# All 48 expert chunks of an image in one stretch behind its attention

## The reference, cut to what matters

```python
# x: 16 images of 192 channels x 32 x 32, so 1024 tokens of 192 channels an image
x = x + L0_conv_ref(_gn(x), ...)     # gated row and column scans, group norm before
t = _to_tokens(x)
t = t + L1_attn_ref(_ln_t(t), ...)   # 6 heads of 32, window of 33 keys, and a first token that sees all and is seen by all
t = t + L1_ffn_ref(_ln_t(t), ...)    # 4 experts, 192 -> 768 -> 192 with gelu; the best 2 of 4 weighted by softmax gates
x = _from_tokens(t, x)
```

## Time and profile before

| | us |
|---|---|
| median of 3 runs (4031.06 to 4038.34) | 4033.3 |
| span of the profiled execution | 4009.3 |
| TensorE busy | 3540.4 (88%) |
| VectorE busy | 2293.3 (57%) |
| ScalarE busy | 1733.3 (43%) |
| mean granted TensorE clock | 0.932 of full |

### The profile page before, as it was taken

The page is one execution under the profiler, slowest core; times in us unless marked ns, Lnnn a source line. Parts: engine busy times, 40 slices in busy tenths (PEclk is TensorE's granted clock), DMA queues, the critical chain, the costliest instruction groups (busy, mean ns, idle before and its releaser), DMA issues.

```text
span 4009.3 us, 68583 instructions
## 1 busy us (share of the span) xinstructions
PE 3540.4 (88%) x24347; PEld 2432.0 (61%) x24347; DVE 2293.3 (57%) x6031; ACT 1733.3 (43%) x4063; POOL 144.9 (4%) x132
## 2 busy tenths in 40 slices
PE   0698989999899899989989998999989989998998
PEld 0466665666666566666656666566666656666665
DVE  3445655656656465655646466564665646565554
ACT  0132634536253363625436263452625336362542
POOL 0000000000000000000000000000000000000000
PEclk9569989999999899999999899998999989999989
DMA  3100000000000000000000000000000000000000
GB/s 48 46 13 4 13 8 13 7 3 14 8 13 8 13 6 4 14 8 14 8 13 6 3 13 8 13 7 2 14 8 13 8 13 6 4 14 8 5 5 9
DMA packets 68306, 44.26 MB, mean 11 GB/s; under 512 B 58909, under 2 KB 59970, under 8 KB 66372
## 3 DMA queue, kind: packets, MB, share of 16 engines
q10 hardware_dynamic: 8416, 30.67, 2.5%
q1 hardware_dynamic: 59492, 8.53, 1.7%
HBM read 21.07 MB, written 12.84 MB: 8 GB/s over the span
## 4 chain that ended last, share of the span: by engine, by line
issue 60%; PE 25%; DVE 8%; POOL 2%; ACT 2%; SPq 0%; DMA 0%; ACTq 0%; POOLq 0%; DVEq 0%
PE PSUM L1137 3%; PE PSUM L1213 2%; PE PSUM L1310 2%; PE PSUM L1134 1%; PE PSUM L1217 1%; PE PSUM L1215 1%; ACT HF L583 1%; PE PSUM L1194 1%; PE PSUM L1195 1%; PE PSUM L1196 1%; PE PSUM L1197 1%; PE PSUM L1198 1%; PE PSUM L1174 1%; DVE X L840 1%; PE PSUM L1230 1%
## 5 line engine op out<-in xcount | busy, mean ns | idle before, releaser
L583 ACT ACTIVATE HF<-PSUM,B 128x512 f32<-128x512 f32 x768 | 509.1, 685 | 732.3 <-PE PSUM L1198 672.0
L1213 PE MATMUL PSUM<-W2H,HHI 128*128 128x192 f16 x3072 | 770.2, 251 | 23.0 <-DVE HLO L828 23.0
L1217 PE MATMUL PSUM<-W2H,HLO 128*128 128x192 f16 x3072 | 765.1, 249 | 0.0
L1215 PE MATMUL PSUM<-W2L,HHI 128*128 128x192 f16 x3072 | 764.8, 249 | 0.0
L825 DVE TENSOR_SCALAR HHI<-HF 128x512 f16<-128x512 f32 x768 | 323.3, 421 | 673.4 <-ACT HF L583 672.5
L828 DVE SCALAR_TENSOR_TENSOR HLO<-HF,HHI 128x512 f16<-128x512 f32 x768 | 531.6, 692 | 26.4
L622 ACT ACTIVATE PS<-PSUM,NMX 94x126 f32<-94x126 f32 x1056 | 366.0, 357 | 114.6 <-DVE NMX L867 77.7
L1213 PEld LDWEIGHTS PSUM<-W2H,HHI 128*128 128x128 f16 x3072 | 313.1, 102 | 132.9 <-issue 41.9
L1230 PE MATMUL PSUM<-KBD,QT 96*94 96x378 f32 x704 | 312.6, 528 | 41.3 <-issue 39.7
L1215 PEld LDWEIGHTS PSUM<-W2L,HHI 128*128 128x128 f16 x3072 | 303.9, 99 | 40.2 <-issue 14.1
L867 DVE TENSOR_REDUCE NMX<-PSUM 94x3 f32<-94x378 f32 x352 | 188.4, 544 | 231.9 <-PE PSUM L1233 207.2
(11 more groups left out here) (233 smaller groups left out, 5542.4 us busy)
## 6 DMA issues: line engine op xcount, KB each, us to landing
XR<-in_x ACTq DMA_DIRECT2D x16, 768.0 KB, 5.6
out_dram<-X ACTq DMA_DIRECT2D x32, 384.0 KB, 2.3
GUP<-TGU SPq DMA_DIRECT2D x256, 8.0 KB, 1.8
TGU<-HSP SPq DMA_DIRECT2D x128, 8.0 KB, 1.8
XG<-HSP SPq DMA_DIRECT2D x128, 8.0 KB, 1.8
HF<-in_w ACTq DMA_DIRECT2D x3, 384.0 KB, 3.3
X<-in_w ACTq DMA_DIRECT2D x3, 384.0 KB, 3.2
XG<-XN SPq DMA_DIRECT2D x16, 64.0 KB, 2.3
```

The lines of the kernel that those rows point to most:

```text
L583: act.activation(HF[:, n % 2, :], PSUM[:, 4 + n % 2, :], ACT.Gelu, scale=1 / (X_UP * W_UP), bias=B1[:, ek:ek + 1]).then_inc(s["gelu_done"], 1)
L1213: pe.matmul(dst, HHI[:, n % 2, tok], W2H[:, e * HK + k, :], start=False, stop=False, skip_group_check=True)
L1215: pe.matmul(dst, HHI[:, n % 2, tok], W2L[:, e * HK + k, :], start=False, stop=False, skip_group_check=True)
L1217: mm = pe.matmul(dst, HLO[:, n % 2, tok], W2H[:, e * HK + k, :], start=False, stop=(k == HK - 1), skip_group_check=True)
```

## The change

All chunks of image i move into `experts(i, *side)`, behind `attention(i)`; `attention` loses its argument `before` and everything that stood under it. `STEPS` becomes one or two side steps a chunk for 8 chunks and one for each later chunk; a new helper `finish` runs out what is left of the generators behind the last chunk. The gates of the second half are made at chunk 26, its route exponential at chunk 24, the first store at chunk 28, the second behind the last chunk. `LINKS_FIRST` is a count of VectorE's own semaphore steps and follows from the order.

```diff
-        STEPS = [(1, n % 2) if n < 17 else (2, 1) for n in range(NCHUNK // 2)] + [(1, 1)]
+        STEPS = [(1, n % 2) if n < 8 else (1, 0) for n in range(NCHUNK)] + [(1, 1)]
+        def finish(works):
+            works = list(works)
+            while works:
+                works = [work for work in works if next(work, works) is not works]
 # ScalarE
-                    if before:
-                        if b == 1:
-                            store(i - 1, 1)
-                        for n in (2 * b, 2 * b + 1):
-                            gelu(i - 1, NCHUNK // 2 + n)
+            def experts(i, *side):
+                step(side, STEPS_AHEAD)
+                for n in range(NCHUNK):
+                    if n == NCHUNK // 2:
+                        route_exp(i, 0)
+                    gelu(i, n)
+                    if n == NCHUNK // 2 + 4:
+                        store(i, 1)
+                    step(side, sum(STEPS[n]))
+                finish(side)
+                store(i, 0)
 # VectorE: split, add_expert and gates leave attention in the same way
+                for n in range(NCHUNK):
+                    if n > 1 and n % HK == 1:
+                        add_expert(i, n // HK - 1)
+                    if n == NCHUNK // 2 + 2:
+                        gates(i, 0)
+                    split(i, n)
+                    step(side, sum(STEPS[n]))
+                add_expert(i, 2 * E - 1)
+                finish(side)
 # TensorE
-                    if before:
-                        ffn1(i - 1, half0 + 2 * b)
-                        ffn1(i - 1, half0 + 2 * b + 1)
                     if b >= 1:
-                        if before:
-                            ffn2(i - 1, half0 + 2 * b - 2)
                         values(2 * b - 2)
                         values(2 * b - 1)
-                        if before:
-                            ffn2(i - 1, half0 + 2 * b - 1)
+            def experts(i, *side):
+                step(side, STEPS_AHEAD)
+                for n in range(NCHUNK + 1):
+                    if n < NCHUNK:
+                        ffn1(i, n)
+                    step(side, STEPS[n][0])
+                    if n >= 1:
+                        ffn2(i, n - 1)
+                    step(side, STEPS[n][1])
+                finish(side)
 # all three engines
-                attention(i, True, True)
-                experts(i, 1, rest(i), conv(i + 1))
+                attention(i, True)
+                experts(i, rest(i), conv(i + 1))
```

More of the change, by code:

```diff
@@ L34 @@
 NCHUNK = NHALF * E * HK
-LINKS_FIRST, LINKS = 78, 61
+LINKS_FIRST, LINKS = 89, 61
 X_UP, W_UP, H_UP = 1024.0, 64.0, 8.0
@@ L608, in route_exp, with attention @@
                 act.activation(SE[:, tiles, :], SC[:, tiles, :], ACT.Exp).then_inc(s["route_exp"], 1)
-            def attention(i, before, following):
+            def attention(i, following):
                 if following:
                     load(i + 1)
-                if before:
-                    route_exp(i - 1, 0)
-                for b in range(NB + 1):
-                    if b < NB:
-                        for n in (2 * b, 2 * b + 1):
[L618 to L625, removed]
-                    if before:
-                        if b == 1:
-                            store(i - 1, 1)
-                        for n in (2 * b, 2 * b + 1):
-                            gelu(i - 1, NCHUNK // 2 + n)
+                for b in range(NB):
+                    for n in (2 * b, 2 * b + 1):
+                        act.wait_ge(s["max_done"], at("max_done", i, n + 1))
+                        if n >= 2:
+                            act.wait_ge(s["pT_done"], at("pT_done", i, n - 1))
+                        for h in range(HH):
+                            e = act.activation(PS[:, n % 2, h, :], PSUM[0:QS, n % 2, h * KS:(h + 1) * KS],
+                                               ACT.Exp, bias=NMX[:, b, n % 2, h:h + 1],
+                                               accum_out=DEN[:, b, n % 2, h:h + 1])
+                        e.then_inc(s["exp_done"], 1)
                 for n in (0, 2):
@@ L653, in rest @@
                 yield
-            def experts(i, half, *side):
+            def experts(i, *side):
                 step(side, STEPS_AHEAD)
-                for n in range(NCHUNK // 2):
-                    gelu(i, (1 - half) * NCHUNK // 2 + n)
+                for n in range(NCHUNK):
[4 more added lines that the diff above has]
+                        store(i, 1)
                     step(side, sum(STEPS[n]))
+                finish(side)
+                store(i, 0)
             def load_weights(n):
@@ L673, in _ @@
                     load_weights(n // 3 + 2)
-            attention(0, False, True)
-            experts(0, 1, rest(0), conv(1))
+            attention(0, True)
+            experts(0, rest(0), conv(1))
             with act.Fori(1, B - 1) as i:
-                attention(i, True, True)
-                experts(i, 1, rest(i), conv(i + 1))
[L679 to L684, removed]
+                attention(i, True)
+                experts(i, rest(i), conv(i + 1))
+            attention(B - 1, False)
+            experts(B - 1, rest(B - 1))
             for half in range(2):
@@ L842, in add_expert, with attention @@
                 last.then_inc(s["ffn_added"], 1)
-            def attention(i, before, following):
-                half0 = NCHUNK // 2
+            def attention(i, following):
                 def copy_turned(n):
@@ L889, in attention @@
                         add_image(i + 1)
-                if before:
-                    split(i - 1, NCHUNK - 2)
                 for n in (1, 3):
@@ L916, in attention @@
                 norm_tokens(X2, range(4, 8)).then_inc(s["xn2_ready"], 1)
-                if before:
-                    add_expert(i - 1, 2 * E - 1)
                 low_parts(i, 1)
@@ L1283, in attention @@
                     turn_output(n)
-                if before:
-                    ffn2(i - 1, NCHUNK - 2)
                 pe.wait_ge(s["oT_copied"], at("oT_copied", i, 4))
@@ L1288, in attention @@
                     output(i, tp)
-                if before:
-                    ffn2(i - 1, NCHUNK - 1)
                 if following:
@@ L1367, in rest, with experts @@
                 yield
-            def experts(i, half, *side):
-                n0 = (1 - half) * NCHUNK // 2
+            def experts(i, *side):
                 step(side, STEPS_AHEAD)
-                for n in range(NCHUNK // 2 + 1):
-                    if n < NCHUNK // 2:
-                        ffn1(i, n0 + n)
+                for n in range(NCHUNK + 1):
+                    if n < NCHUNK:
+                        ffn1(i, n)
                     step(side, STEPS[n][0])
                     if n >= 1:
-                        ffn2(i, n0 + n - 1)
+                        ffn2(i, n - 1)
                     step(side, STEPS[n][1])
+                finish(side)
             for part in (group_mean, group_variance, project_states):
```

19 lines of the change are left out of this document (removed).

## The result

The changed kernel takes 4679.8 us (median of 4 runs, 4677.1 to 4686.6) against 4032.2 us: ratio 1.163, 95% interval 1.159 to 1.167, so 16% slower. The forecast was 4640 us, slower by 15%, range 4480 to 4765.

The account below looks back on a forecast made before the run. TensorE was taken to bound attention and expert stretches at nearly full clock. Attention -14.0 and experts +54.8 gave +40.8 us a usual image, +607 in all; 4009.3 + 607 + 24.0 gave 4640 us, range 4480 to 4765.

Parts of the forecast that it names:

- Attention without chunks, 89.0 + 3.9 = 92.9: Usual attention at low clock: image 0's 89.0 us plus 3.9 for blocks 0 to 2 redone; -14.0 against 106.9.
- The sign that I had named for the order on ScalarE: Sign of a wrong forecast: TensorE waiting over 5 us at L1230 behind the last chunk, from store or load order.
- so it is hidden as well: Next image's load, queued behind the last store, costs nothing: its first reader L724 comes some 13 us after the last chunk.
- 53.7 us of chunks: Expert stretch: 24 chunks at 2.06 us put in, plus 4.2 for bias matmuls, all on TensorE; +53.7 us an image.
- -5.9 by spreading: Expert stretch: waits before the mixing (3.0) and for `add_expert` (2.9) go at one side step a chunk; bounds 0 and -5.9.
- +7.0 of new waits: Expert stretch: bare last chunks and border 2.3, gates 2.3, low clock 2.4; together +7.0 us an image.
- The gates: VectorE's linked operations at chunk 26, ahead of the split, make TensorE wait 2.3 us, bounds 1 and 3.3.
- The sum: Images 2 to 14 at +40.8 us, image 0 +54.8, image 1 +39.4, image 15 -17.1: together +607.
- The 24 us around the span: 24.0 us of time outside the traced span, added to the forecast span of 4616 us to give 4640.
- The rival of the full clock: Clock stays up or returns in attention, blocks 4.09 us: 377 us less, 4263 us in all; chance 0.10.
- Bare blocks at TensorE's own pace: Attention blocks take 3.2 us at full clock and spreading removes 12 us of waits: about 3921 us, faster; chance 0.04.
- More low clock in the expert stretch: Clock stays low behind attention into more images' expert stretches, 9 us more each, 126 in all: 4766 us; chance 0.12.

Follow-up runs that it names:

- a dense order in the changed kernel: Changed kernel with the side steps of the kernel before, all side work done by chunk 20 and 27 bare chunks after: 4858.0 us, ratio 1.210.
- matmuls in each block: Changed kernel, all images but the first: 16 unread matmuls in block 0, 4 ahead of each later block's values (10 in block 2): 4305.8 us, ratio 1.073.
- spread statistics: Changed kernel with 16 unread matmuls in block 0 and VectorE's four next-image L722 one a block, their norm three blocks later: 4335.6 us, ratio 1.079.
- the control: The changed kernel unaltered, timed once more beside other runs on its chip: 4684.7 us against 4023.3 for the kernel before, ratio 1.166.
- one burst: Changed kernel with 16 unread 512-column matmuls behind the scores of block 0, in every image but the first: 4588.5 us, ratio 1.143.
- the store later: Changed kernel with the second half's store moved behind the exponentials of block 0 of the next attention: 4623.5 us, ratio 1.152.

## Why the prediction was right, point by point

*Attention without chunks, 89.0 + 3.9 = 92.9.* Right in mechanism: low from the loop's way back to L1078's matmuls, 90.5 us of 95.2 at 1.2 GHz, blocks of 6.4 us. Too small by 2.3: block 0 took 6.2 us (2178.04 - 2171.85) where I took 3.3, for the 2.76 us wait for the first exponentials. The sign that I had named for the order on ScalarE, over 5 us of waiting behind the last chunk, came in two parts, 3.05 and 2.76. The step that failed is "so it is hidden as well" on the load behind the last store: I had priced the load's reader on VectorE, and not ScalarE's own program, which stands behind that store.

*53.7 us of chunks.* No run measures them alone. The stretch of image 0 grew from 126.2 to 177.0, +50.8, but it also lost 10 us of low clock (17.1 to 6.8); with low time counted at half, an estimate, it grew by 56. Between image 5 before and image 7 after it is 61.2 us, of which the listed waits are +1.5, the loop's way back -0.5 and the low clock about +4.7; that leaves some 55.

*-5.9 by spreading.* The sized step that was wrong: the earlier trace rows's two went from 5.9 to 5.7 in all, with 1.4 new (L1133). What spreading does give, 11.4 us, is against a dense order in the changed kernel, which I did not need.

*+7.0 of new waits.* The gates cost nearly nothing: TensorE's wait at the border of chunk 24 is 0.78 us, and there is none at chunk 26, where I took 2.3. The low clock took its place: over image 7's stretch 0.95 of 187.9 us is some 19 us low, against some 10 in image 5 before, so about 4.5 us where I took 2.4. As a mean of images 2 to 14 it hardly changed, 16.4 to 18.1 us, since before some images had 28 or 42 us of it; that is why the mean grew by 57.7 and not by 61.2.

*The sum.* An image +46.1 instead of +40.8, 13 times 5.3 = 69 us; images 0, 1 and 15 came to +50.7, +34.6 and -13.9 instead of +54.8, +39.4 and -17.1. That makes 13 x 46.1 + 71 = 670, and 666 in the spans (4675.3 - 4009.3), since the first attention begins 3.3 us earlier, against 607. Images 1 and 15 began at full clock, but TensorE waited 3.47 and 3.10 us for the first exponentials and the clock fell there: attentions of 95.0 and 92.0 us where I took 89.0 and 86.0. In image 15, without L1078, the clock then stayed low for 105.6 us, 18 of them in its expert stretch. The 24 us around the span was a mistake that hid part of it: the profiled execution after took 4677.1 us with a span of 4675.3, so 1.8 us lie around it, and the profiled execution before was faster than the median of its runs (those of the kernel before lie between 3981 and 4046 us in all that I timed). With 1.8 the forecast would have been 4618 us, 62 too low instead of 40; that the two errors went against each other was luck.

*The rival of the full clock.* Priced at 377 us, 25.4 an image. It did not happen by itself, but made to happen in part it gave 374 us (matmuls in each block) and 349 (spread statistics against the control). That 374 and 377 lie so close is partly luck: the attentions of images 2 to 14 gave 21.4 us each where I had 25.4, and the rest came from images 1 and 15 and from 2.5 us an expert stretch that I had not counted. So of the 661 us by which the control is slower than the kernel before on its chip, a little over half at least is clock. The rest, 312 us (4335.6 - 4023.3) to 340 us (4341.8 - 4001.4), still holds low clock: 38 and 34 us of each attention in these two runs, 19 in the one with matmuls in each block. An estimate of what is left without it: had images 2 to 14 of that run taken the 66.6 us of its image 1, it would be 13 x 7.3 = 95 us shorter, some 4210 us, 200 over the kernel before. The rows of the kernel before say the same: its attentions take 106.8 us, 40.2 more than the 66.6, for 24 chunks of 53.7 us, so some 13.5 us an image lay beside a block's waits, 15 x 13.5 = 200 us. No run measured that share by itself.

*The other rivals.* Bare blocks at TensorE's own pace took 3.2 us a block and an attention under 65 us; at full clock a block takes 3.83 us, with a wait of 0.51 us in it, and the attention 66.6. More low clock in the expert stretch did not come: 18.1 us against 16.4.

*Two slips that change no term.* The clock strip of the earlier trace rows is low in the second slice too, and the full clock's four parts add up to 67.3 us, not 67.5.

*The Trainium skill's rule* (TensorE: Matmul & The Clock Gate, Part 1) that activity releases the throttle did not hold for the activity of a bare attention: TensorE was busy 87.7 of 95.1 us at a clock of 0.53. It held for the burst. Part 4 of the same page of the Trainium skill says that transposes don't count as busy in the same way. Whether this is why the bare blocks never rose stays open; blocks with all their transposes kept the full clock in the run with spread statistics, and the six turns of a block took 0.65 us there against 1.15 at the low clock.

## What to carry to other kernels

Work taken from between operations that wait for each other can be paid twice, as here: by its own length elsewhere and by the clock that it kept up. Look for a stretch of the old trace that has no such work and read its block time and granted clock. A single wait in a thin stretch can cost far more than itself (2.24 us here, and 1.03 in another run, each followed by 34 us or more at half the clock), so spread what causes it, or fill it with dense matmuls into a free bank, and check where the clock falls next. When a store or load moves behind a last dependency, ask what its engine's own program does next, the way round the loop included.

## What the runs showed of the hardware

- The clock of a bare attention has two lasting courses. At 1.2 GHz it stays there for 72 to 92 us, and for 105.6 in image 15, with TensorE busy 92 to 97% of the time. At 2.4 GHz it stayed there for 34 us with spread statistics and for 45.6 us, all 11 blocks of image 15, with one burst; in these blocks a pair of scores (0.85 us) comes every 3.83 us, with a wait of 0.51 us in each.
- Waits of 2.30, 2.24, 1.49 and 1.03 us in bare blocks came with a fall from 2.4 to 1.2 GHz, or just ahead of it, while in the dense expert stretch of image 5 waits of 3.10, 2.03 and 2.86 us did not bring it down. During 16 matmuls of 512 columns in block 0 it rose again.
- Adding 66 matmuls to each attention but the first made the changed kernel 8% faster (4305.8 against 4679.8 us).
- The loop's way back costs TensorE about 3 us (3.05) and ScalarE some 4.6 us between its last DMA issue and its first of the next turn. With ScalarE's last store waiting for the last `add_expert`, TensorE idled 3.05 and then 2.76 us; with the store later, 3.2 and 0.8.
